# Pair loops of a conditioned transformer block written out as straight code on all five engines

## What is computed

```
h   = film(rmsnorm(x, norm1_w), cond, film1_w, film1_b)    # h*(1+scale)+shift, scale and shift from cond
Q, K, V = h @ q_w + q_b, h @ k_w + k_b, h @ v_w + v_b
attn = softmax(Q K^T * 512**-0.5)
x   = x + (attn @ V) @ proj_w + proj_b
h   = film(rmsnorm(x, norm2_w), cond, film2_w, film2_b)
out = x + gelu(h @ mlp_w1 + mlp_b1) @ mlp_w2 + mlp_b2      # 512 -> 2048 -> 512
```

## Time and profile before

| what | value |
|---|---|
| median of the runs | 1980.09 us (three runs: 1980.07, 1980.09, 1985.26) |
| span of the profiled execution, first to last instruction | 1981.4 us, 1.3 us above the median |
| TensorE busy | 1930.8 us, 8870 matmuls |
| VectorE, ScalarE, GpSimd busy | 729.5, 679.9, 345.3 us |
| mean granted TensorE clock | 0.995 of full speed |
| setup and attention pass | 0 to 568.5 us |
| MLP pass | 568.5 us to the end |

### The profile page before, as it was taken

The page is one execution under the profiler, slowest core; times in us unless marked ns, Lnnn a source line. Parts: engine busy times, 40 slices in busy tenths (PEclk is TensorE's granted clock), DMA queues, the critical chain, the costliest instruction groups (busy, mean ns, idle before and its releaser), DMA issues.

```text
span 1981.4 us, 23941 instructions
## 1 busy us (share of the span) xinstructions
PE 1930.8 (97%) x8870; PEld 1603.2 (81%) x8870; DVE 729.5 (37%) x1286; ACT 679.9 (34%) x1387; POOL 345.3 (17%) x354
## 2 busy tenths in 40 slices
PE   9889999999899999999999999999999999999999
PEld 8777887878788888887888788788878878888887
DVE  6765657566643222322222232222222232222211
ACT  4334434444343333333233233233333323233322
POOL 1452433424364010110101010110101010110100
PEclk9999999999999999999999999999999999999999
DMA  8323132331431101101010111101010110101000
GB/s 300 116 76 128 64 127 91 100 126 65 138 107 54 54 12 53 54 18 48 22 49 16 55 33 32 54 19 46 22 51 15 54 50 16 53 22 45 20 22 22
DMA packets 86969, 121.07 MB, mean 61 GB/s; under 512 B 13664, under 2 KB 39264, under 8 KB 86880
## 3 DMA queue, kind: packets, MB, share of 16 engines
q1 hardware_dynamic: 86880, 119.75, 18.8%
HBM read 70.41 MB, written 33.55 MB: 52 GB/s over the span
## 4 chain that ended last, share of the span: by engine, by line
PE 88%; DVE 8%; issue 3%; ACT 1%; DMA 0%; SPq 0%; POOL 0%; DVEq 0%; ACTq 0%; POOLq 0%
PE score L464 21%; PE pT L464 18%; PE ring L641 12%; PE ring L645 12%; PE ring L642 12%; PE ring L464 5%; DVE h L826 4%; PE ring L547 3%; PE ring L546 3%; PE ring L550 3%; DVE xT_in L818 1%; PE ring L501 1%; DVE pT_lo L1010 1%; DVE top L986 0%; DMA wkT<-wkT_dram 0%
## 5 line engine op out<-in xcount | busy, mean ns | idle before, releaser
L1047 DVE TENSOR_TENSOR act_lo<-act_full,act_hi 128x512 fp32r<-128x512 f32 x256 | 189.6, 740 | 987.2 <-ACT act_full L768 987.1
L641 PE MATMUL ring<-w_hi,act_hi 128*128 128x512 f32 x1020 | 397.1, 389 | 0.0
L642 PE MATMUL ring<-w_lo,act_hi 128*128 128x512 f32 x1020 | 396.9, 389 | 0.0
L645 PE MATMUL ring<-w_hi,act_lo 128*128 128x512 f32 x1020 | 272.6, 389 | 0.0
L767 ACT ACTIVATE act_hi<-score,vecs 128x512 fp32r<-128x512 f32 x128 | 88.3, 690 | 498.5 <-PE score L464 498.5
L767 ACT ACTIVATE act_hi<-pT,vecs 128x512 fp32r<-128x512 f32 x128 | 88.3, 690 | 457.8 <-PE pT L464 457.7
L641 PEld LDWEIGHTS ring<-w_hi,act_hi 128*128 128x128 f32 x1020 | 191.5, 188 | 39.8
L645 PEld LDWEIGHTS ring<-w_hi,act_lo 128*128 128x128 f32 x1020 | 191.5, 188 | 39.7
L642 PEld LDWEIGHTS ring<-w_lo,act_hi 128*128 128x128 f32 x1020 | 191.6, 188 | 39.5
L464 PE MATMUL score<-h_lo,w_hi 128*128 128x512 f32 x512 | 199.9, 390 | 8.1 <-issue 8.1
L464 PE MATMUL score<-h_hi,w_hi 128*128 128x512 f32 x512 | 199.9, 391 | 5.6 <-issue 5.5
(11 more groups left out here) (142 smaller groups left out, 2789.9 us busy)
## 6 DMA issues: line engine op xcount, KB each, us to landing
x_in<-x_dram SPq DMA_DIRECT2D x64, 256.0 KB, 3.4
xT_in<-xT_dram SPq DMA_DIRECT2D x16, 1024.0 KB, 6.8
x_scratch<-x_in SPq DMA_DIRECT2D x64, 256.0 KB, 2.1
x_in<-x_scratch SPq DMA_DIRECT2D x64, 256.0 KB, 3.8
out_dram<-x_in SPq DMA_DIRECT2D x64, 256.0 KB, 2.3
h_half<-blocks SPq DMA_DIRECT2D x480, 32.0 KB, 1.9
stage<-w_dram SPq DMA_DIRECT2D x32, 256.0 KB, 2.7
f2w<-f2w_dram SPq DMA_DIRECT2D x1, 2048.0 KB, 15.6
```

The lines of the kernel that those rows point to most:

```text
L641: pe.matmul(ring[b][:], act_hi[r][:, tokens(b)], w2_hi[:, j, :], start=j == 0, stop=False)
L642: pe.matmul(ring[b][:], act_hi[r][:, tokens(b)], w2_lo[:, j, :], start=False, stop=False)
L645: mm = pe.matmul(ring[b][:], act_lo[r][:, tokens(b)], w2_hi[:, j, :], start=False, stop=j == KH - 1)
L1047: dve.tensor_tensor(act_lo[r][:], act_full[r][:], act_hi[r][:].bitcast(F32), ALU.subtract).then_inc(act_lo_done[r], 1)
```

## The change

`group_pairs` calls the bodies in a plain Python loop over all eight pairs. All sixteen groups of both passes are written out on all five engines, the register expressions become constants, and there is no jump back. The order of the instructions that do work is the same.

```diff
 def group_pairs(engine, pairs, body):
 
 
-    for p in range(2):
-        body(p, p, 0)
-    with engine.Fori(1, pairs - 1) as i:
+    for i in range(pairs):
         for p in range(2):
             body(2 * i + p, p, i)
-    for p in range(2):
-        body(2 * (pairs - 1) + p, p, pairs - 1)
```

## The result

The changed kernel takes 1993.08 us (median of 8 runs, 1989.49 to 1994.08) against 1979.82 for the kernel before, run beside it (median of 8); the ratio is 1.0066 [1.0044, 1.0088]. It is slower by 0.7%, where 1.0% faster was forecast, with 0.03 on any slower outcome. The profiled span grew from 1981.4 to 1992.2 us, by 10.8.

A forecast was written before the change was run, and what follows sets the result against it. TensorE, busy 97% of the 1981.4 us span, was taken as the bound. Gains of 16.5 (MLP back edges) and 3.0 (attention register waits) summed to 19.5 us: span 1961.9, median 1960.6, range 1952 to 1969.

The forecast's parts named there:

- (a): MLP pass, TensorE: straight code removes five back edges of 3.2 to 3.5 us; gain 16.5 us, bounds 13 and 17.5.
- (c): MLP pass, TensorE: waits against constants instead of registers gain 0.
- (e): MLP pass, VectorE, ScalarE, GpSimd: their losses in register waits and jumps cost nothing now; gain nothing.
- (b): Attention pass back edges: removing them gains 0, at most 0.01 us each.
- (d): Attention pass: constant waits save 0.17 us before scaling x, 0.08 after pT_lo; 3.0 us over 12 loop groups, bounds 0 and 15.
- (f): SyncE: its addresses become constants; 0 on either side, as no wait of TensorE ends with a DMA.
- (g): Instruction fetch: TensorE streams attention too, 18 packets, and other engines fetch all along; cost taken as 0.
- rivals on fetches: Exposed instruction fetches of VectorE and ScalarE (1990.6 us), or TensorE streaming stalls in attention (1976 us).
- Two or three exposed fetches: Attention pass, VectorE and ScalarE: two or three fetches stall the path, giving 1965 to 1967 us; chance 0.12 (1965 to 1971).
- TensorE's own streaming stalls: Attention pass: 18 packets at 0.87 us idle each cost 16 us, result 1976; chance 0.07, shared with more exposed fetches.
- second rival: Attention speeds up more: all 0.9 us idle goes per group, product starts warm; 31.5 us gain, median 1948.6; chance 0.12.
- slower rival: Attention pass: 14 exposed VectorE and ScalarE fetches of 2.15 us cost 30, median 1990.6; chance 0.03 for slower than 1986.

The follow-up runs named there:

- VectorE alone: The kernel before with VectorE's attention pass alone written straight, all else in its loops: 1975.77 us, 0.9978 of the kernel before.
- two reductions: The kernel before with two added idle VectorE reductions in each looped attention group, between scaling and modulation, copy untouched: 2011.60 us, 1.0134.

## Why the prediction was wrong

- *(a), the MLP back edges*: right, 16.5 us, and with it (c) and (e): the MLP stretches are 174.08 us with and without a former back edge. (b), nothing for attention's back edges, also held: without them and without the hold, groups come 30.9 us apart with and without a former back edge.
- *(d), register waits in attention, 3.0 us*: right by size where nothing else intervenes. Without ScalarE's straight code the groups come 30.91 us apart instead of 31.15, the step behind the copy is 0.02 and the wait 0.67. VectorE alone gives 31.00. The rest, 0.08, is the step from the end of pT_lo to the first product: 0.12 us with VectorE alone, 0.04 where TensorE is straight too. The changed kernel has both savings as well: copy 1.17 and exp_bias 0.08 us longer, less 0.25, is the 1.0 us by which its wait grew.
- *(f), (g), and the rivals on fetches*: no wait of any engine between 130 and 520 us is put down to issue. The queue of large packets carried 70 (forecast 70 to 78), the other 35 (16 before, where "several times as many" was forecast), and the only wait of TensorE that is put down to issue in the whole span is one of 0.2 us at 62 us. "Two or three exposed fetches" and "TensorE's own streaming stalls" did not occur.
- *The step that failed* is in (d): "Everything between these steps keeps its length". It took the durations of VectorE's small instructions as their own. They were not: exp_bias took 0.56 us in the looped groups and 0.23 in group 0, and this was in the trace; it was held by GpSimd, and the copy, right behind it, was free of the hold only because it came in a gap. ScalarE's straight code, with its fourth sum 0.06 us later, closed the gap: the copy took 1.34 us, and the wait that was to fall from 0.91 to 0.65 rose to 1.92. The sentence against the second rival, "I found no other step of the chain that differs between it and group 6", was wrong too. Group 14, straight before, has a longer exp_bias than the looped groups (0.62 against 0.56 us, row below), which shows that its length was not its own (GpSimd does other work there, so the row does not give the size):

```profile
515.88 0.62 DVE L988 TENSOR_SCALAR exp_bias<-top 128x4 f32<-128x4 f32 x1
```

- *What was left out around it.* The port stood in (d) only as a reason for winning nothing, not as one for losing. I weighed what each engine would save and asked of each whether it had slack, but not whom its shifted work would meet. ScalarE's part was filed under slack.
- *Nor did I price the clock.* My bounds for a longer wait would have been its length. Once TensorE waits 1.9 us here, ten of twelve groups cost 1.55 us on top, more than the hold itself (1.17).
- *The slower rival* ended on the right side through the wrong mechanism: it was worked out for fetches. That its 1990.6 lies near the 1993.08 measured is luck, and its chance doesn't count for what happened.

What stays open: why ScalarE's fourth sum starts 0.06 us later in straight code (its waits are the same in number, against constants), and what decides at the boundary of two adds. No run took these apart.

## What to carry to other kernels

Before a change that shifts engines against each other by even a tenth of a microsecond, look for small instructions on the path whose duration differs between groups (0.17 here, 0.56 there): another engine may be holding them, and their neighbours are at risk. Take them off the path (an earlier copy) and take the other engine's work away from it: both together took the span from 1959.8 us, straight code with no hold of the copy, to 1942.5. Then write out code whose jump back costs TensorE time. Price a wait of TensorE by what stands behind it as well: here 1.5 us of idle time cost 1.5, and 2.1 cost 3.7 in eleven groups of twelve.

## What the runs showed of the hardware

- A VectorE instruction with one SBUF source (the 128x32 copy, the 128x4 tensor-scalar) that meets GpSimd's 128x512 add of 1.26 us is held until that add ends, unless it gets in at the boundary of two adds: 1.34 against 0.17 us, 0.56 to 0.72 against 0.17. The maximum of the scores, which reads PSUM, and the scaling of x, which reads x^T in SBUF and the spread rows in PSUM, kept 0.69 and 2.48 us (four) beside the same adds. The Trainium skill (GPSIMD Engine Reference, "8. Key points") says that GpSimd shares its SBUF interfaces with VectorE, with contention for instructions in a 2-port mode or with two SBUF inputs; the two held instructions, with one SBUF source each, could only be of the first kind. The runs agree in which instructions are held; that they run in a 2-port mode no run shows. The hold lasted to the end of the add, however short the held instruction was.
- A jump back to a body of about 310 matmuls and as many weight loads cost TensorE nothing; to one of 769 and 769 it cost 3.2 to 3.5 us in two stalls. Straight code streamed both without a stall.
- TensorE's clock: idle for 0.91 and 1.54 us once in each group, it stayed at the higher level in all twelve groups; idle for 1.92 us it fell in 10 of 12, for 2.13 and 2.18 us (two reductions; ScalarE alone straight) in 11 of 12. In group 4 of the changed kernel it fell 1.04 us after work had begun again (219.05 to 220.09), in the others 0 to 1.6 us after.
